# Other piece ends for the products over the counts: 512, 896 and 1250 in ten of twelve blocks

## The reference

```
def gcn_conv(x, W, b, src, dst, n_nodes):
    h = x @ W
    deg = segment_sum(ones_like(dst), dst)
    dinv = where(deg > 0, rsqrt(deg), 0.0)
    norm = dinv[src] * dinv[dst]
    msgs = h[src] * norm[:, None]
    out = segment_sum(msgs, dst)
    return out + b
...
h = relu(gcn_conv(n, W1, b1))
out = gcn_conv(h, W2, b2)
x = layernorm(x + out)
```

## Time and profile before

| | us |
|---|---|
| median of 3 runs | 809.3 (807.68 to 810.53) |
| the profiled execution | 808.74 |
| its span in the trace | 807.0 |
| PE busy | 771.1 (96%) |
| DVE busy | 578.3 (72%) |
| ACT busy | 321.2 (40%) |

### The profile page before, as it was taken

One profiled execution on the slowest core, in us unless ns is written; L12 is line 12 of the kernel. 1 busy time (PEld: TensorE's weight loads), 2 busy tenths in 40 slices (PEclk: granted clock), 3 DMA queues, 4 the chain that ended last, 5 costly groups with the idle time before them and its releaser, 6 DMA issues.

```text
span 807.0 us, 11730 instructions
## 1 busy us (share of the span) xinstructions
PE 771.1 (96%) x4215; PEld 645.5 (80%) x4215; DVE 578.3 (72%) x1133; ACT 321.2 (40%) x638; POOL 23.4 (3%) x38
## 2 busy tenths in 40 slices
PE   5999999999999989999999998899999999999997
PEld 4966666665665989999965788798789998889996
DVE  2599987886899999999689999794643332403554
ACT  4537666654533434343253555562203331301000
POOL 6100000000000010000000020000000000000000
PEclk9999999999989999999989999999999999999999
DMA  9400000000000132010000510100000003000121
GB/s 311 160 2 1 1 1 2 1 1 2 1 1 0 67 132 66 1 66 1 1 0 1 183 31 2 41 1 1 1 1 1 1 1 117 1 1 1 59 78 55
DMA packets 10672, 28.15 MB, mean 35 GB/s; under 512 B 675, under 2 KB 4079, under 8 KB 10100
## 3 DMA queue, kind: packets, MB, share of 16 engines
q1 hardware_dynamic: 10612, 27.36, 9.8%
HBM read 23.48 MB, written 3.88 MB: 34 GB/s over the span
## 4 chain that ended last, share of the span: by engine, by line
PE 82%; DVE 11%; ACT 3%; issue 2%; DMA 1%; SPq 1%; DVEq 0%; ACTq 0%
PE ps L1221 78%; DVE att L689 4%; DVE att L728 4%; PE ps L1320 1%; PE ps L1374 1%; DMA edges<-in_dst 1%; PE ps L1263 1%; DVE out L712 1%; ACT att L1053 0%; DVE h2x L712 0%; ACT uB L911 0%; DVE ylo_a L830 0%; ACT ctr L911 0%; PE ps L1508 0%; ACT xT L936 0%
## 5 line engine op out<-in xcount | busy, mean ns | idle before, releaser
L1221 PE MATMUL ps<-g,att 128*128 128x193 f32 x800 | 133.4, 328 | 3.2 <-DVE att L689 1.7
L1221 PEld LDWEIGHTS ps<-g,att 128*128 128x128 f32 x800 | 130.3, 190 | 6.1 <-DVE att L689 3.1
L1053 ACT ACTIVATE att<-att,ssrc 128x1250 f32<-128x1250 f32 x60 | 80.1, 1338 | 97.1 <-DVE att L728 96.9
L1221 PE MATMUL ps<-ctr,yhi 128*128 128x512 f32 x360 | 89.9, 357 | 1.8 <-DVE ylo_b L830 1.4
L728 DVE SCALAR_TENSOR_TENSOR att<-uB,s 128x1250 f32<-128x1250 f32 x60 | 90.6, 1514 | 0.0
L1221 PE MATMUL ps<-wp,xT 128*128 128x388 f32 x240 | 87.5, 502 | 0.8 <-ACT xT L936 0.8
L689 DVE SCALAR_TENSOR_TENSOR att<-att,ct 128x1250 f32<-128x1250 f32 x60 | 87.2, 1454 | 1.5 <-ACT att L1053 1.3
L830 DVE TENSOR_TENSOR ylo_a<-ps,yhi 128x512 fp32r<-128x512 f32 x24 | 15.4, 685 | 83.0 <-ACT yhi L911 83.0
L1221 PE MATMUL ps<-ctr,ylo_a 128*128 128x512 f32 (+1 forms) x288 | 71.1, 355 | 0.1
L1221 PEld LDWEIGHTS ps<-ctr,yhi 128*128 128x128 f32 x360 | 59.7, 188 | 12.6 <-DVE ylo_b L830 1.7
L1221 PEld LDWEIGHTS ps<-wp,xT 128*128 128x128 f32 x240 | 42.6, 190 | 24.8 <-issue 1.0
(11 more groups left out here) (250 smaller groups left out, 1369.1 us busy)
## 6 DMA issues: line engine op xcount, KB each, us to landing
uB<-u_dram SPq DMA_DIRECT2D x4, 1280.0 KB, 6.1
wux<-in_L_gnn_Wu SPq DMA_DIRECT2D x2, 2304.0 KB, 16.3
gw<-in_L_gnn_W SPq DMA_DIRECT2D x2, 2304.0 KB, 10.3
xs<-in_x SPq DMA_DIRECT2D x1, 3456.0 KB
out<-ybuf SPq DMA_DIRECT2D x9, 384.0 KB, 2.3
w<-in_L_gnn_W SPq DMA_DIRECT2D x2, 1152.0 KB, 6.9
w2x<-in_L_gnn_W SPq DMA_DIRECT2D x1, 576.0 KB, 7.6
wuo<-in_L_gnn_Wu SPq DMA_DIRECT2D x1, 576.0 KB
```

Of the source, the lines that this page charges most:

```text
L1053: a.activation(at_, at_, ACT.Exp, bias=ssrc[:, h, q:q + 1]).then_inc(att_exp, 1)
L1221: return t.matmul(o, lhsT, rhs, start=start, stop=stop, **kw)
```

## The change

A second list, SPANS, ends the pieces at 512, 896 and 1280. Blocks 2 to 5 of the first convolution (`a_spans`) and all six of the second (`b_spans`) use it; blocks 0 and 1 of the first keep PIECES. In these ten blocks every product but those of the first triple ends at column 1250: the last piece is 384 columns wide in the first triple (q = 0, high part) and 354 in the other 19. So a triple of 512, 512 and 256 columns becomes one of 512, 384 and 354. The number of products, loads, banks and semaphores is as before. The last piece now holds the row tiles 7, 8 and 9, of which 7 lies in `ylo_a` and 8 and 9 in `ylo_b`, so `sums_low` needs two DVE instructions for it, four per block. The waits of the weight products look their piece up in the new lists: tile 7 now belongs to the third.

```diff
+SPANS = [(0, 512), (512, 896), (896, NP)]
...
+        def a_spans(f):
+            return PIECES if f < 2 else SPANS
...
+        def b_spans(f):
+            return SPANS
...
-        def lo_rows(k, f):
-            c0, c1 = PIECES[k]
-            a0, a1 = c0 // P, c1 // P
-            return (ylo_a[:, a0:a1] if a0 < YA else ylo_b[:, a0 - YA:a1 - YA])[:, :, f * P:(f + 1) * P]
+        def lo_rows(span, f):
+            a0, a1 = span[0] // P, span[1] // P
+            return ([(a0, min(a1, YA), ylo_a[:, a0:min(a1, YA), f * P:(f + 1) * P])] if a0 < YA else []) + (
+                [(max(a0, YA), a1, ylo_b[:, max(a0, YA) - YA:a1 - YA, f * P:(f + 1) * P])] if a1 > YA else [])
...
-                    for k in range(3):
+                    for k, span in enumerate(spans(f)):
                         v.wait_ge(hi_out, 3 * f + k + 1)
-                        c0, c1 = PIECES[k]
-                        v.tensor_tensor(lo_rows(k, f), place(f, k).rearrange("p (t n) -> p t n", n=P),
-                                        yhi[:, c0 // P:c1 // P, f * P:(f + 1) * P].bitcast(F32), ALU.subtract).then_inc(done, 1)
+                        for a0, a1, rows in lo_rows(span, f):
+                            last = v.tensor_tensor(rows, place(f, k)[:, a0 * P - span[0]:a1 * P - span[0]].rearrange("p (t n) -> p t n", n=P),
+                                                   yhi[:, a0:a1, f * P:(f + 1) * P].bitcast(F32), ALU.subtract)
+                        last.then_inc(done, 1)
...
-                        for k, (c0, c1) in enumerate(PIECES):
+                        for k, (c0, c1) in enumerate(a_spans(f)):
                             if q == 0 and n == 0:
                                 t.wait_ge(alo_out, freed(A_BANKS, 3 * f + k, A_BANKS[f][k]) if f >= 2 else 0)
-                            last = mm(a_place(f, k), part(q, f * P, (f + 1) * P), counts[:, q, c0:c1], q == 0 and n == 0 and (f, k) != (1, 2), final,
+                            if f >= 2 and (q > 0 or n > 0):
+                                c1 = min(c1, N)
+                            last = mm(a_place(f, k)[:, 0:c1 - c0], part(q, f * P, (f + 1) * P), counts[:, q, c0:c1], q == 0 and n == 0 and (f, k) != (1, 2), final,
...
-                            for k, (c0, c1) in enumerate(PIECES):
+                            for k, (c0, c1) in enumerate(b_spans(f)):
                                 if q == 0 and n == 0 and f >= 2:
                                     t.wait_ge(blo_out, freed(B_BANKS, 3 * f + k, B_BANKS[f][k]))
-                                last = mm(b_place(f, k), part(q, f * P, (f + 1) * P), counts[:, q, c0:c1], q == 0 and n == 0, final)
+                                if q > 0 or n > 0:
+                                    c1 = min(c1, N)
+                                last = mm(b_place(f, k)[:, 0:c1 - c0], part(q, f * P, (f + 1) * P), counts[:, q, c0:c1], q == 0 and n == 0, final,
+                                          skip_group_check=True)
```

More of the change, by code:

```diff
@@ L347, in att_place @@
             return (n + NA - EARLY) % NA
+        def a_spans(f):
+            return PIECES if f < 2 else SPANS
+        def b_spans(f):
+            return SPANS
         def a_place(f, k):
-            c0, c1 = PIECES[k]
+            c0, c1 = a_spans(f)[k]
             first = 256 if (f, k) == (1, 2) else 0
@@ L355, in b_place @@
         def b_place(f, k):
-            c0, c1 = PIECES[k]
+            c0, c1 = b_spans(f)[k]
             return ps[:, B_BANKS[f][k], 0:c1 - c0]
@@ L823, in message_low, with sums_low @@
                     v.scalar_tensor_tensor(ylo(q, 0, D), xs[:, q, :], dinv[:, q:q + 1], y(q, 0, D), ALU.mult, ALU.subtract).then_inc(zlo_out, 1)
-                def sums_low(f, place, hi_out, done):
-                    for k in range(3):
+                def sums_low(f, place, spans, hi_out, done):
+                    for k, span in enumerate(spans(f)):
                         v.wait_ge(hi_out, 3 * f + k + 1)
-                        c0, c1 = PIECES[k]
-                        v.tensor_tensor(lo_rows(k, f), place(f, k).rearrange("p (t n) -> p t n", n=P),
-                                        yhi[:, c0 // P:c1 // P, f * P:(f + 1) * P].bitcast(F32), ALU.subtract).then_inc(done, 1)
+                        for a0, a1, rows in lo_rows(span, f):
+                            last = v.tensor_tensor(rows, place(f, k)[:, a0 * P - span[0]:a1 * P - span[0]].rearrange("p (t n) -> p t n", n=P),
+                                                   yhi[:, a0:a1, f * P:(f + 1) * P].bitcast(F32), ALU.subtract)
+                        last.then_inc(done, 1)
                 v.wait_ge(x_added, 2 * T)
@@ L845, in messages @@
                 for f in range(KD):
-                    sums_low(f, a_place, ahi_out, alo_out)
+                    sums_low(f, a_place, a_spans, ahi_out, alo_out)
                     if f == 2:
@@ L873, in messages @@
                 for f in range(KD):
-                    sums_low(f, b_place, bhi_out, blo_out)
+                    sums_low(f, b_place, b_spans, bhi_out, blo_out)
                     if f == 1:
@@ L1178, in messages, with sums_high @@
                             done += 1
-                def sums_high(f, place, sums_ps, done, last):
+                def sums_high(f, place, spans, sums_ps, done, last):
                     a.wait_ge(sums_ps, last)
-                    for k, (c0, c1) in enumerate(PIECES):
+                    for k, (c0, c1) in enumerate(spans(f)):
                         if place is a_place and (f, k) == (1, 2):
@@ L1189, in messages @@
                 for f in range(KD):
-                    sums_high(f, a_place, a_ps, ahi_out, max(3 * f + 3, 6))
+                    sums_high(f, a_place, a_spans, a_ps, ahi_out, max(3 * f + 3, 6))
                 for n in range(2 * T):
@@ L1201, in messages @@
                 for f in range(KD):
-                    sums_high(f, b_place, b_ps, bhi_out, 3 * f + 3)
+                    sums_high(f, b_place, b_spans, b_ps, bhi_out, 3 * f + 3)
                     if f == 1:
@@ L1578, in first_layer @@
                         if n == 0 or c == KD - 1:
-                            t.wait_ge(alo_out, 3 * c + 1 + next(m for m, (_, c1) in enumerate(PIECES) if q * P < c1))
+                            t.wait_ge(alo_out, 3 * c + 1 + next(m for m, (_, c1) in enumerate(a_spans(c)) if q * P < c1))
                         split_product(ps[:, H_RING[n % 4], 0:HALF], (yhi[:, q, c * P:(c + 1) * P], ylo(q, c * P, (c + 1) * P)),
@@ L1606, in second_layer @@
                         if n == 0 or c == KD - 1:
-                            t.wait_ge(blo_out, 3 * c + 1 + next(m for m, (_, c1) in enumerate(PIECES) if q * P < c1))
+                            t.wait_ge(blo_out, 3 * c + 1 + next(m for m, (_, c1) in enumerate(b_spans(c)) if q * P < c1))
                         split_product(ps[:, F_RING[n % 4], 0:HALF], (yhi[:, q, c * P:(c + 1) * P], ylo(q, c * P, (c + 1) * P)),
```

## The result

The changed kernel takes 806.0 us in the median of 22 runs, beside 808.17 for the kernel before in the same measurement; the ratio is 0.9965 with a 95% interval of 0.9954 to 0.9977. The ratio stands for 2.8 us (1.9 to 3.7) less and the two medians lie 2.2 us apart, where 2.4 were forecast. A second measurement gave 0.9977 (0.9958 to 0.9997). So the time fell, and whether it fell by more than 0.3% is open: both intervals hold 0.997. The profiled execution has a span of 804.9 us, against 807.0.

What follows compares the result with a forecast made beforehand. PE's stream was taken to bound the kernel; gains of 1.47, 0.49, 0.19 and 0.22 us sum to 2.37 us, so 809.3 - 2.4 = 806.9 us for the median, range 805.0 to 809.5.

Steps and rivals of the forecast that it cites:

- What bounds the kernel: PE's stream, 82% of the chain of waits; after 543.88 us two PE runs around a short ACT and DVE detour.
- handover: Detour over ACT and DVE between blocks 2 and 3, 566.84 to 570.75 us: 3.85 us, PE busy 2.06, expected to stay.
- The terms: Gains at 12.9 ns per clipped triple: second convolution 1.47, first's blocks 4 and 5 0.49, block 3 0.19, block 2 0.22 us.
- The boundary is worth nothing by itself: Moving the boundary from 1024 to 896 gains nothing; only the 30 columns of padding count, 12.9 ns per clipped triple.
- The linear law: A PE product costs a fixed some 10 ns plus 0.43 ns per column, taken from distances between starts.
- Rival 1: Below 384 columns the weight load sets PE's pace, 175 ns between starts; gain nil, 809.3 us; chance 0.05.
- Rival 2: Lighter handover at 567 to 571 us drops PE's clock to 1.2 GHz, losing 1.7 us: 808.6 us; chance 0.03.
- Rival 3: Products of 354 columns miss float32r's fast rate, 152 ns more per clipped triple: about 836 us; chance 0.04 with other losses.
- DVE is covered: The fourth subtraction costs DVE 145 ns per block, 1.45 us in all, hidden in idle time without PE waiting.

Runs made afterwards that it cites:

- the deferred version: Changed kernel with block 2's row tiles 6, 7 and 8 moved behind `pair(9)`: 803.98 us, ratio to before 0.9946; measured again 803.69 us, 0.9945.
- finer subtractions: Changed kernel with one low-part subtraction per tile of 128 in blocks 2 to 5, in both branches: 810.57 us, ratio to before 1.0029.
- longer untaken code: Changed kernel with subtractions cut per tile only in the untaken branch for wide counts, 48 more DVE instructions, none executed: 809.75 us, ratio to before 1.001.
- 256 columns: Changed kernel with products clipped at column 1152 instead of 1250, new boundaries kept, last piece 256 wide, some sums left out: ratio to before 0.9858.

## Why the prediction was right, point by point

- **What bounds the kernel.** PE's stream, in two runs with one handover. The chain of the changed kernel has the same links, and the deferred version shows that the handover was a true wait. I had it at 3.85 - 2.06 = 1.8 us; it was worth 2.65.
- **The terms.** Second convolution: 1.47 forecast, 69.68 - 68.17 = 1.51 measured. Blocks 3 to 5: 0.68 and 34.49 - 33.79 = 0.70. Block 2: 0.22 and 22.96 - 22.73 = 0.23. Sum 2.37 and 2.44. The medians (2.2 us) and the ratio (2.8, from 1.9 to 3.7) lie on both sides of that and need no further cause.
- **The boundary is worth nothing by itself.** Right, ratio 1.001. But I took from it that the 30 columns are the only thing that matters, and this step fell as a general statement: without the new boundary the clipping gives 2.4 ns a triple instead of 13. The linear law was fitted to widths of 256 and more and I carried it below. That the forecast didn't suffer is because 354 columns lie within the fitted widths. The clipping is worth its 13 ns only with the boundary, which lifts the last piece off the floor.
- **Rival 1**, a pace set by the load. It exists, but at about 115 ns, not at the 175 at which I priced it. The shown 188 ns of a load are not its cost, any more than a product's shown duration is: loads follow each other after 108 ns. The 81 ns at 128 columns that the Trainium skill gives (TensorE: Matmul & The Clock Gate, section Back-to-back issue gap) are not seen either; here it is 115.
- **Rival 2**, the clock after the handover. It stayed 1.00 in the changed kernel, and fell in three other profiled executions (finer subtractions, longer untaken code, 256 columns), at about 1.5 us (1.52 and 1.55 in the first two), close to the 1.7 I had put on it. The changed kernel's lighter handover isn't needed for it: with the longer untaken code PE executes the same instructions there as in the changed kernel, and the clock fell in one and not in the other.
- **Rival 3**, a slow rate for odd widths. Fell: 354, 226 and 128 columns all run at the rate of their width or at the floor.
- **DVE is covered.** Right, with five times the instructions that the change adds. The price was too high: I put 145 ns on an instruction, from shown durations, and 1.45 us on all; by the starts it is some 65 ns, and DVE's busy time grew by 0.7 us. What I had not looked at is that more instructions also mean more code. The change adds ten to each branch and pays nothing; 48 more in the untaken branch cost more than the change had gained (1.001 instead of 0.9965).

## What to carry to other kernels

Get a product's cost from distances between starts at several widths, and use the law only between the widths it was fitted to. Do the same for a wait before pricing it: the span of the wait less what its products cost in a dense stretch. Cut padding from a piece only when it stays wider than its weight load takes (here some 250 columns for a load of 128, an estimate from 118 ns at 256 columns and 0.43 ns per column), and even out the pieces first if it doesn't. When an added instruction seems covered but the time moves, compare the first instruction of each branch in the two timelines before blaming the work.

## What the runs showed of the hardware

- A float32r product with its own 128-column load never counted less than about 115 ns: 120 at 256 columns, 118 at 226, 115 at 128. The starts of two loads behind a short product lay 108 or 109 ns apart at both 128 and 226 columns. In the trace the short product looks short (223 ns at 128 columns) and the one behind it long (448 instead of 392).
- DVE's subtractions from PSUM overlap: shown 281 ns long at 128 columns, the next one starts after 198; at 384 columns 548 and 464.
- DVE's first instruction in a branch came with 2.4 us of idle time and no releaser in two kernels whose untaken branch was 48 instructions longer, and waited only for ACT, 0.7 to 1.2 us, in the other ten profiled executions. Why the place of the code decides wasn't tried.
- After the handover, in which PE was half idle (busy 2.03 of 3.85 us in the changed kernel), the granted clock stayed 1.00 in some executions and fell in others that do the same work there (0.60 in the mean of 573 to 577 us with the longer untaken branch), at some 1.5 us a time.
